# GATv2 pass of a graph network: the one-hot of a step's nodes is made by POOL, one per step, in place of VectorE, eight steps at once

## What is computed

```
x_l = x @ W_l + b_l
x_r = x @ W_r + b_r
h = x_l[src] + x_r[dst]
h = jnp.where(h >= 0, h, 0.2 * h)
e = h @ att
e_max = segment_max(e, dst)
alpha = jnp.exp(e - e_max[dst])
denom = segment_sum(alpha, dst)
out = segment_sum((alpha / (denom[dst] + 1e-16))[:, None] * x_l[src], dst) + bias
```

## Time and profile before

| | us |
|---|---|
| median of three timed runs | 4729.43 |
| lowest and highest of them | 4728.7, 4730.91 |
| span of the profiled execution | 6520.0 |
| VectorE busy in it | 3179.2 |
| POOL busy in it | 3300.8 |
| TensorE busy in it | 3657.4 |
| ScalarE busy in it | 2465.9 |

### The profile page before, as it was taken

The page is one execution under the profiler, slowest core; times in us unless marked ns, Lnnn a source line. Parts: engine busy times, 40 slices in busy tenths (PEclk is TensorE's granted clock), DMA queues, the critical chain, the costliest instruction groups (busy, mean ns, idle before and its releaser), DMA issues. The chain is left out here.

```text
span 6520.0 us, 95479 instructions
## 1 busy us (share of the span) xinstructions
PE 3657.4 (56%) x21401; PEld 3175.1 (49%) x21402; DVE 3179.2 (49%) x8146; ACT 2465.9 (38%) x5473; POOL 3300.8 (51%) x3507
## 2 busy tenths in 40 slices
PE   3555555555622223326576777778666666666665
PEld 2444444444512222225466666666455555555555
DVE  4555555555613323326566666666543443434435
ACT  4444444444400000003566666663433333333334
POOL 4444545454375666663566666652344444444442
PEclk6555555555655565567788888889776666676666
DMA  5222222222121111111444444543121111111112
GB/s 112 55 57 54 58 54 58 54 57 55 30 58 38 45 46 46 45 45 56 138 148 148 147 148 149 150 142 92 40 50 45 46 45 45 45 46 47 45 45 51
DMA packets 367219, 462.19 MB, mean 71 GB/s; under 512 B 104067, under 2 KB 271235, under 8 KB 367104
## 3 DMA queue, kind: packets, MB, share of 16 engines
q0 software_dynamic: 107648, 226.35, 15.1%
q1 hardware_dynamic: 255344, 232.90, 11.8%
q10 hardware_dynamic: 4112, 1.71, 0.1%
HBM read 327.40 MB, written 134.06 MB: 71 GB/s over the span
## 5 line engine op out<-in xcount | busy, mean ns | idle before, releaser
L898 POOL DMA_INDIRECT v_G<-dr_tab,src_idx x832 | 794.3, 955 | 1008.6 <-ACT v_RH L1511 784.1
L898 POOL DMA_INDIRECT e_G<-dr_tab,src_idx x832 | 796.0, 957 | 836.9 <-DVE e_RH L1196 593.3
L898 POOL DMA_INDIRECT m_G<-dr_tab,src_idx x832 | 786.5, 945 | 508.9 <-PE m_OUT L2127 271.2
L1798 POOL DMA_INDIRECT s_G<-dr_tab,chunk_src x784 | 741.1, 945 | 398.9 <-issue 228.9
L1886 PE MATMUL s_OUT<-s_G,s_S 128*128 x1664 | 348.7, 392 | 829.7 <-issue 522.9
L1886 PEld LDWEIGHTS s_OUT<-s_G,s_S 128*128 128x128 f32 x1664 | 321.9, 296 | 856.4 <-issue 856.4
L1842 DVE TENSOR_TENSOR ACC<-ACC,s_OUT 128x129 f32 x832 | 240.8, 289 | 750.2 <-remote 491.8
L2045 DVE TENSOR_TENSOR ACC<-ACC,m_OUT 128x256 f32 x832 | 347.2, 417 | 472.2 <-DMA dr_step_rows<-tail 358.8
L1310 PE MATMUL e_OUT<-e_RH,e_S 128*128 128x144 f32 x1664 | 512.6, 477 | 1.9 <-DVE e_RH L1196 1.9
L1496 ACT COPY v_NXS<-v_NX 128x512 f32<-128x512 f32 x208 | 121.9, 586 | 1012.6 <-remote 722.1
L2126 PE MATMUL m_OUT<-m_G,m_S 128*128 128x128 f32 x1664 | 413.5, 336 | 139.6 <-issue 107.7
(11 more groups left out here) (382 smaller groups left out, 8991.5 us busy)
## 6 DMA issues: line engine op xcount, KB each, us to landing
dr_ends<-m_XB SPq DMA_DIRECT2D x416, 256.0 KB
e_LR<-dr_row_loc SPq DMA_DIRECT2D x104, 256.0 KB
m_MS<-dr_row_start SPq DMA_DIRECT2D x104, 256.0 KB
v_LR<-dr_row_loc SPq DMA_DIRECT2D x104, 256.0 KB
e_G<-dr_tab,src_idx POOLq DMA_INDIRECT x832
m_G<-dr_tab,src_idx POOLq DMA_INDIRECT x832
v_G<-dr_tab,src_idx POOLq DMA_INDIRECT x832
s_G<-dr_tab,chunk_src POOLq DMA_INDIRECT x784
```

The source lines that it names most:

```text
L898: pool.indirect_dma_start(out=out, out_offset=None, in_=table, in_offset=bass.IndirectOffsetOnAxis(ap=g["src_idx"][:, step:step + 1], axis ...
L1798: pool.indirect_dma_start(out=G[:, c % (RING * GROUP), 0:D], out_offset=None, in_=table[:, :], in_offset=bass.IndirectOffsetOnAxis(ap=g["c ...
```

## The change

The one-hots leave VectorE's body. POOL makes one 128x128 one-hot per step, behind the gather of that step, with tensor_scalar (is_equal against the step's column of loc) from iota_row in SBUF. Behind the first gather of a group POOL waits for mm_done of group k - 4, as S is now a ring of four groups of 4 KB a partition each. s_done counts steps, and TensorE waits for eight of them a group. The values in S are the same.

```
-        S = sb("S", [P, 2, GROUP, P])
+        S = sb("S", [P, 4, GROUP, P])
...
                     for s in range(GROUP):
                         gather_step(g, pool, table[:, :], G[:, b, s, 1:AC + 1], k * GROUP + s, gathered[b])
+                        if s == 0:
+                            wait(pool, mm_done, GROUP * (k - 3))
+                        step = k * GROUP + s
+                        pool.tensor_scalar(S[:, b, s, :], g["iota_row"][:], g["loc"][:, step:step + 1], None,
+                                           ALU.is_equal).then_inc(s_done, 1)
...
-                def onehots(k, b):
-                    wait(dve, mm_done, GROUP * (k - 1))
-                    V.tensor_tensor(S[:, b % 2], *onehot_rows(nodes, g["loc"], k), ALU.is_equal).then_inc(s_done, 1)
...
                     over_steps(k, i, b)
-                    onehots(k, b)
                     maxima(k, b)
...
-                        pe.wait_ge(s_done, k + 1)
+                        pe.wait_ge(s_done, GROUP * (k + 1))
...
-                        nc.tensor.matmul(OUT[:, s // 3, (s % 3) * AC:(s % 3 + 1) * AC], S[:, b % 2, s, :], RH[:, s, :],
+                        nc.tensor.matmul(OUT[:, s // 3, (s % 3) * AC:(s % 3 + 1) * AC], S[:, b % 4, s, :], RH[:, s, :],
...
-                        sums(k - 1, b + 1, range(0, 3))
+                        sums(k - 1, (b + 3) % 4, range(0, 3))
...
-                        sums(k - 1, b + 1, range(3, GROUP))
+                        sums(k - 1, (b + 3) % 4, range(3, GROUP))
```

## The result

The changed kernel takes 5231.4 us (median of four runs, 5228.1 to 5233.54) against 4730.17 us before: ratio 1.1058, interval 1.1044 to 1.1071, 501 us more. Forecast were 248 us more and a range that ended at 5200. Two repetitions gave 1.1057 [1.1038, 1.1075] and 1.106 [1.1041, 1.1078].

The account below looks back on a forecast made before the run. The prediction took POOL's back-to-back gathers, 10.0 us a group, as the bound. Eight one-hots of 0.31 us add 2.48 us in 100 groups: 4729 + 248 = 4977 us, own range 4845 to 5110, stated range 4800 to 5200.

Parts of the forecast that it names:

- POOL is the bound, gathers back to back: Kernel before: 3280 gathers x 1.25 us plus 681.5 us rest make 4782 us; 10.0 us a GATv2 group, slack taken as 0.
- 1791 us of the profile are time that the timed runs don't have: Profiled span 6520.0 us against timed median 4729.43 us; idle time in the trace was to be read with care.
- The chain of the others, 9.1 to 10.7 us: GATv2 group: the engines other than POOL need 9.1 to 10.7 us a group, depending on TensorE's speed level.
- Removal costs and gains nothing, as L1690 covers it: VectorE's 1214 ns one-hot per group is covered by TensorE's last-row transpose and what follows, so removing it counts as nothing.
- The price of the one-hot on POOL: Each 128x128 tensor_scalar behind a gather costs 310 ns, interpolated from TENSOR_SCALAR rows; 2.48 us a group, 248 us over 100 groups.
- Wrong on the cost if they take 0.6 us: Sign to check in the profile after: POOL's 832 TENSOR_SCALAR were expected near 0.3 us each.
- Rival (a): The compare is slow on POOL: 0.78 us each gives 624 us more, 5353 us; chance 10%.
- The first four groups hidden, 9.9 us: Start of the GATv2 pass: four groups' one-hots, 4 x 2.48 us, hide in POOL's 24.2 us idle waiting for RH.
- The added wait is met in time: POOL's wait for mm_done of group k-4: round trip 12.0 us a group, just under POOL's own 12.5 us.
- rival b: POOL's one-hots are held up by VectorE instructions with two SBUF operands: at most 77 us on top, 5054 us; chance 6%.
- rival c: POOL's slack or the 0.30 us before each gather hides most of the one-hots' cost: 4729 to 4824 us; chance 12%.
- Rival (d): VectorE's chain is the bound, not POOL, so removing its one-hot gains up to 125 us, 4604 us; chance 5%.

Follow-up runs that it names:

- b_again: The kernel before, unchanged, timed and profiled once more on a chip where it takes about 4730 us: 4729.87 us, ratio 0.9998.
- half_gathers: The kernel before with four gathers a group instead of eight in the GATv2 pass, odd steps working on ones: 4730.5 us, ratio 0.9997.
- cols32: The changed kernel with POOL's one-hot on 32 of 128 columns, on the chip where the kernel before takes 6535 us: 6069.86 us, ratio 0.9287.
- no_onehots: The kernel before with VectorE's one-hots made for the first two groups only, nothing put on POOL: 4731.42 us, ratio 0.9999.
- half_no_onehots2: The kernel before with four gathers a group and no VectorE one-hots after the second group, on a common chip: 4730.33 us, ratio 0.9996.
- pool_dummy: The kernel before, VectorE's one-hots kept, plus POOL's eight tensor_scalar a group into an unread spare tile, without waiting for mm_done: 5230.97 us, ratio 1.1052.
- form3: The kernel before plus one POOL multiply-then-add per step, two immediates, 3 columns, into an unread tile: 4840.11 us, ratio 1.0231.
- imm_mult: The changed kernel with mult by an immediate instead of is_equal with a pointer, on the chip where the kernel before takes 6535 us: 6268.06 us, ratio 0.9594.
- mult: The changed kernel with mult in place of is_equal, pointer kept, on the chip where the kernel before takes 6535 us: 6253.7 us, ratio 0.9569.

## Why the prediction was wrong

**POOL is the bound, gathers back to back: half right.** b_again shows 1.249 us from start to start and hardly any slack, so that work added to POOL is paid in full, which is what the forecast needed. But with half the gathers the time stays (half_gathers, 4730.5), so the timed kernel is bound by POOL and by the chain of the others alike. The sum by which I came to it (3280 x 1.25 plus the rest) used a rest from the slower chip: 681.5 us, where b_again has 600 outside its four passes. With it the sum is 4700 us, 0.6% below the measured time, and not 4782.

**"1791 us of the profile are time that the timed runs don't have": wrong in its cause.** I put them down to the profiler. The same kernel takes 6535 us unprofiled on one chip, and a profile from another has a span of 4728.8 us. Profiled executions are as long as the others on either chip: cols32 has a span of 6071.5 us beside a median of 6069.86. The expected span of 6520 to 6650 us with a nearly unchanged look was wrong with it: 5226.3.

**The chain of the others, 9.1 to 10.7 us: right**, 10.04 by half_gathers.

**Removal costs and gains nothing, as L1690 covers it: right** (no_onehots, half_no_onehots2). The idle before L1592 grew by 1.1 us a group, 1.2 were forecast.

**The price of the one-hot on POOL: the step that failed.** "I take 310 ns, the interpolated one with a little for the pointer: same operation, same engine, one input." The opcode was the same, the arithmetic in it was not. For multiply-then-add with a pointer the number is right, 0.318 us in the step. For is_equal it is 0.605, so the term of 100 groups x 8 x 0.31 = 248 us should have been about 500. The prediction's own sign, "Wrong on the cost if they take 0.6 us", is what the profile shows: 0.63. The affine select, which compares, stood there at 780 ns, named as the upper bound; between ends that far apart I chose by the opcode's name. Rival (a) came nearest, with too high a price (0.78) and not quite the right reason: a lone multiply is as dear as the compare.

**The first four groups hidden, 9.9 us: wrong in cause, nearly right in size.** The 24.2 us of the earlier trace rows aren't there on the common chip, but waits of 7.9 and 1.0 us are.

**The added wait is met in time: right.** POOL waits for nothing, and pool_dummy without that wait costs the same.

**Held up by VectorE (rival b): only at the start**, 9.0 us over 16 steps against 4.4 before, and not the 77 us of the rival. **Hidden in the 0.30 us (rival c): not so**, though a part is: the gather's lead falls to 0.17 us, and form3, an instruction of 0.21 us, adds 0.134. **Rival (d): fell.**

**The sum** with the measured price: 831 x 0.605 = 503 us, less 8.3 for the two waits that are filled and plus 4.6 for the longer start, is 499 us. 4730 + 499 = 5229, measured 5231.

## What to carry to other kernels

Price an instruction that the trace doesn't show by a row with the same arithmetic operations, not only the same opcode and shape; where the nearest rows differ there, keep the far end inside the range. Where one engine's queue is full end to end, any work added to it costs its growth of the step times the count, and a removal elsewhere gives nothing. Before calling one engine the bound, ask what is left when its work is halved: here the answer was the same time. When the profiled span and the timed median are far apart, think of another chip as well as of the profiler (here it was the chip), and forecast for the one that was timed.

## What the runs showed of the hardware

POOL's tensor_scalar on 128 columns of f32 adds 0.239 us between two gathers as multiply-then-add with immediates, 0.318 with a pointer (and the one-hot's tiles), 0.605 as is_equal with a pointer, 0.715 as is_equal-then-mult with a pointer and 0.749 with immediates. The length shown isn't the price: imm_mult was shown with 0.53 us and mult with 0.63, at steps of 1.868 and 1.844.

A gather of 128 rows costs POOL 1.249 us on either chip, yet one chip took 38% more for the kernel before, and there kernels with more POOL work (mult, imm_mult) were 4% faster. In their traces the gathers are evenly spaced; that this is the reason is not shown.
